# A four-layer perceiver in one launch: L1 and L2 self-attention written out tile by tile, and the L0 alignment and L0 attention reordered

## Time and profile before

| | |
|---|---|
| median of 3 runs | 4878.07 us (4868.13 to 4886.44) |
| the profiled execution | 4887.39 us, span 4885.7 us |
| mean granted TensorE clock | 0.884 of 2.4 GHz |
| busy: PE, PEld, DVE, ACT, POOL | 75%, 61%, 73%, 58%, 21% of the span |
| L0 cross attention (distances and alignment) | 17.2 to 486.1 us |
| L0 attention | 486.1 to 616.6 us |
| L1 attention | 1586.4 to 1735.3 us |
| L2 attention | 2736.6 to 2886.8 us |

### The profile page before, as it was taken

One profiled execution on the slowest core, in us unless ns is written; L12 is line 12 of the kernel. 1 busy time (PEld: TensorE's weight loads), 2 busy tenths in 40 slices (PEclk: granted clock), 3 DMA queues, 4 the chain that ended last, 5 costly groups with the idle time before them and its releaser, 6 DMA issues. The chain is left out here.

```text
span 4885.7 us, 68656 instructions
## 1 busy us (share of the span) xinstructions
PE 3687.9 (75%) x23747; PEld 2956.0 (61%) x23747; DVE 3576.9 (73%) x5812; ACT 2810.2 (58%) x4595; POOL 1036.9 (21%) x993
## 2 busy tenths in 40 slices
PE   6236617999999567999999765777777777777775
PEld 3235315999998345899999532555555555555664
DVE  4675776787776432877787447999999999997443
ACT  3112404666665322666666314998988999997112
POOL 0000402111210200221111111444434444443000
PEclk9556757999999779999999877999999999998777
DMA  7452001111110001111110001000000000000000
GB/s 272 69 81 70 1 5 59 35 35 35 35 35 9 7 18 61 34 35 34 36 35 21 9 5 37 14 24 18 14 14 28 14 14 28 14 8 19 1 0 15
DMA packets 182323, 158.33 MB, mean 32 GB/s; under 512 B 7340, under 2 KB 170364, under 8 KB 182012
## 3 DMA queue, kind: packets, MB, share of 16 engines
q1 hardware_dynamic: 175356, 138.02, 10.2%
q10 hardware_dynamic: 6656, 16.38, 1.1%
HBM read 127.62 MB, written 20.20 MB: 30 GB/s over the span
## 5 line engine op out<-in xcount | busy, mean ns | idle before, releaser
L537 PEld LDWEIGHTS psU<-ctxN,ST 128*128 128x128 f32 x6656 | 853.8, 191 | 98.0 <-issue 39.2
L537 PE MATMUL psU<-ctxN,ST 128*128 128x129 f32 x6656 | 868.0, 275 | 20.5 <-issue 20.5
L1159 DVE MAX8 top<-pairs 128x8 f32<-128x801 f32 (+1 forms) x512 | 709.1, 1406 | 4.5
L623 ACT ACTIVATE ST<-ST 128x512 f32<-128x512 f32 (+1 forms) x832 | 513.3, 625 | 166.9 <-DVE ST L725 162.9
L934 PE MATMUL psU<-ctxN,PT 128*128 128x129 f32 (+1 forms) x3328 | 432.9, 281 | 201.2 <-ACT PT L1042 201.1
L1124 POOL TENSOR_TENSOR P<-P,EX 128x1601 f32<-128x1601 f32 x128 | 459.5, 3589 | 586.8 <-ACT P L1034 586.8
L725 DVE TENSOR_TENSOR ST<-ST,psB 128x512 f32<-128x512 f32 (+1 forms) x832 | 556.2, 677 | 3.3 <-PE psB L556 3.3
L711 DVE TENSOR_TENSOR psA<-psA,ST 128x512 f32<-128x512 f32 x640 | 446.5, 698 | 136.7 <-ACT ST L615 69.6
L934 PEld LDWEIGHTS psU<-ctxN,PT 128*128 128x128 f32 (+1 forms) x3328 | 395.3, 193 | 225.5 <-ACT PT L1042 225.5
L1164 DVE MATCH_REPLACE8 pairs<-top,pairs 128x801 f32<-128x801 f32 (+1 forms) x384 | 482.3, 1256 | 0.0
L912 PE MATMUL psS<-KT,stat 128*128 128x512 f32 (+1 forms) x1024 | 389.4, 524 | 15.9 <-DVE pairs L1143 15.1
(11 more groups left out here) (459 smaller groups left out, 6731.6 us busy)
## 6 DMA issues: line engine op xcount, KB each, us to landing
ctxT<-ctxT_scratch SPq DMA_DIRECT2D x48, 800.5 KB, 4.7
ctxN<-in_ctx SPq DMA_DIRECT2D x48, 768.0 KB
ctxT_scratch<-trn ACTq DMA_DIRECT2D x16, 800.5 KB
nat<-in_ctx SPq DMA_DIRECT2D x16, 768.0 KB
ctx<-in_ctx SPq DMA_DIRECT2D x16, 768.0 KB
dist_scratch<-dd SPq DMA_DIRECT2D x8, 800.5 KB
room<-dcol SPq DMA_DIRECT2D x28, 201.0 KB, 4.2
dcol<-dist_scratch SPq DMA_DIRECT2D x16, 201.0 KB, 16.7
```

The lines of the kernel that those rows point to most:

```text
L537: last = pe.matmul(psU[:, q, 0:D + 1], ST[0:n, i % SLOTS, q * 128:q * 128 + 128], ctxN[0:n, j, k, 0:D + 1], start=(k == 0 and q % 2 == 0), ...
L623: act.activation(ST[0:n, i % SLOTS, :], ST[0:n, i % SLOTS, :], ACT.Exp).then_inc(exp_done, 1)
L1159: dve.max(top[:, j, 8 * n:8 * n + 8], pairs[:, j, 0:width]).then_inc(listed, 1)
```

## The change

1. **Distances**: for a group of 512 columns PE first issues the token products of both batches, then waits once for both squares, then issues the two matmuls of ones.
2. **Alignment, opening**: only the parts of `dcol` that no DMA fills are set to zero, all by DVE. Of POOL's work only `top` stays in the opening block; `same_batch`, `iota_far` and `place` go to POOL in the block of the steps.
3. **Alignment, rows**: one ring of 36 rows and one more. `carry_row` is run once, at step 36, in place of 17 times.
4. **Alignment, last sums**: the two batches of a tile take turns, product by product, into the two halves of the partitions.
5. **L0 attention**: the keys of tile t+2 go ahead of `mix(t)` on POOL; ACT negates the maxima; ACT copies the values, behind `key_squares(1)`, in place of DVE; POOL makes `group_rows`; DVE takes key and query forms half by half; the first dots and denominators go ahead of the values on PE; each waits for its half of the queries only. For the last tile DVE multiplies, masks, finds the maximum and subtracts it, and ACT takes one exponential for 8 heads.
6. **L1 attention** has a function of its own, `attention_gelu`, and **L2 attention** another, `attention_wide_values`, both written out for 8 tiles, with scores two tiles ahead, three buffers of `P`, and the keys spread over 8 groups of heads on two halves of the partitions. In L2 the weights are applied to x itself (4 matmuls a tile, 64-row stationary, 512 columns), and the weight is multiplied once a tile (16 matmuls, accumulated). In L1 the heads are summed transposed, so gelu takes its bias from the partition and feeds the projection directly; two tiles share a gelu. Half of the products need x or V with its two batches exchanged, which SP makes by DMA. L3 keeps `small_attention`.

```diff
 # distances
                         for j in range(2):
                             b = 2 * p + j
-                            r = slice(j * S, j * S + S)
-                            pe.wait_ge(squared, b + 1 + ONE)
-                            pe.matmul(psD[r, n, 0:w], xm2[:, b * S:b * S + S], trn[:, b % TURNS, o:o + w],
+                            pe.matmul(psD[j * S:j * S + S, n, 0:w], xm2[:, b * S:b * S + S], trn[:, b % TURNS, o:o + w],
                                       start=True, stop=False)
-                            last = pe.matmul(psD[r, n, 0:w], c.ones[:, 0:S], trn_sq[:, b % TURNS, o:o + w],
+                        pe.wait_ge(squared, 2 * p + 2 + ONE)
+                        for j in range(2):
+                            b = 2 * p + j
+                            last = pe.matmul(psD[j * S:j * S + S, n, 0:w], c.ones[:, 0:S], trn_sq[:, b % TURNS, o:o + w],
                                              start=False, stop=True)
 # alignment
-                    dve.memset(dcol[:, 0:STEPS // 2, :], 0.0).then_inc(filled, 1)
+                    dve.memset(dcol[:, 0:BLOCKS - 1, :], 0.0).then_inc(filled, 1)
+                    dve.memset(dcol[:, S:STEPS, :], 0.0).then_inc(filled, 1)
+                    dve.memset(dcol[:, BLOCKS - 1:S, 0:1], 0.0).then_inc(filled, 1)
+                    dve.memset(dcol[96:128, BLOCKS - 1:S, 1 + FROM[-1][1]:ROWS + 1], 0.0).then_inc(filled, 1)
...
-                            if s % G == 0 and s:
-                                pe.wait_ge(row_carried, s // G + ONE)
+                            if s == RING:
+                                pe.wait_ge(row_carried, 1 + ONE)
...
-                for b in range(B):
...
+                for p in range(NT):
...
                     for k, (o, w) in enumerate(KC):
                         pe.wait_ge(inside_ready, g * len(KC) + k + 1 + ONE)
-                        last = pe.matmul(psX[r, b // 2, :], inside[0:w, k, b * S:b * S + S], ctx[0:w, b, k, :],
-                                         start=(k == 0), stop=(k == len(KC) - 1))
+                        for j in range(2):
+                            b = 2 * p + j
+                            last = pe.matmul(psX[j * S:j * S + S, p, :], inside[0:w, k, b * S:b * S + S],
+                                             ctx[0:w, b, k, :], start=(k == 0), stop=(k == len(KC) - 1))
 # L0 attention: POOL, then ACT
-                for t in range(NT):
-                    mix(t)
+                for t in range(NT - 1):
                     if t + 2 < NT:
                         keys(t + 2)
+                    mix(t)
...
+                def negate(t):
+                    act.wait_ge(max_found, t + 1 + ONE)
+                    act.activation(nmx[:, t % 2, :], mx[:, t % 2, :], ACT.Copy, scale=-1.0).then_inc(neg_ready, 1)
 # L2 attention, new: PE's order, and two of its steps
+                def values(t):
+                    pe.wait_ge(pt_ready, 2 * t + 2 + ONE)
...
+                    for b in range(2):
+                        for e in range(2):
+                            n = 2 * b + e
...
+                            x = c.xn if b == e else swapped
+                            pe.matmul(u_bank(n), x[rows(e), t, :], PT[rows(e), t % 2, :, rows(b)], start=True, stop=True
+                                      ).then_inc(u_ready, 1)
+
+                def output(t):
+                    pe.wait_ge(ut_ready, 4 * t + 4 + ONE)
...
+                    for h in range(H):
+                        last = pe.matmul(psY[:], UT[:, t % 2, h // 2, h % 2].rearrange("p b s -> p (b s)"), W[:, h, :],
+                                         start=(h == 0), stop=(h == H - 1))
...
+                scores(0)
+                scores(1)
+                for t in range(NT):
+                    if t + 2 < NT:
+                        scores(t + 2)
+                    turn(t)
+                    if t:
+                        output(t - 1)
+                    values(t)
+                output(NT - 1)
 # L1 attention, new: the sums of a tile, PE's loop, DVE's two passes and DVE's loop
+                    for a in range(8):
+                        for b in range(2):
+                            for e in range(2):
+                                h = 2 * a + e
+                                v = V if b == e else swapped
+                                r = slice(h % 4 * 32, h % 4 * 32 + 32)
+                                last = pe.matmul(psO[r, h // 4, t % 2, rows(b)], v[rows(e), t, h * 32:h * 32 + 32],
+                                                 PT[rows(e), t % 2, a, rows(b)], start=True, stop=True)
...
+                for t in range(NT):
+                    if t + 2 < NT:
+                        scores(t + 2)
+                    turn(t)
+                    if t + 2 < NT:
+                        values(t + 2)
+                    if t >= 3 and t % 2:
+                        output(t - 3)
+                        output(t - 2)
+                    sums(t)
...
+                    dve.tensor_tensor(p, psS[:].rearrange("p g (h k) -> p (g h) k", k=S), bc(mask[:], [128, H, S]), ALU.add
+                                      ).then_inc(masked, 1)
...
+                    dve.reduce_max(m[:, :, 0], p, axis=X).then_inc(max_ready, 1)
...
+                    dve.tensor_tensor(p, p, bc(m, [128, H, S]), ALU.subtract).then_inc(sub_ready, 1)
...
+                    dve.reduce_sum(m[:, :, 0], p, axis=X).then_inc(sum_ready, 1)
...
+                    dve.reciprocal(m[:, :, 0], m[:, :, 0]).then_inc(inv_ready, 1)
...
+                    dve.tensor_tensor(p, p, bc(m, [128, H, S]), ALU.mult).then_inc(p_ready, 1)
...
+                for t in range(NT):
+                    if t + 2 < NT:
+                        shift(t + 2)
+                    if t + 1 < NT:
+                        weigh(t + 1)
+                    if t >= 3 and t % 2:
+                        add(t - 3)
+                        add(t - 2)
```

More of the change, by code:

```diff
@@ L1852, in _ @@
                     project(n)
-                values(0)
-                values(1)
                 dots(0)
@@ L1857, in _ @@
                     far(0, part)
-                values(2)
-                values(3)
+                for p in range(4):
+                    values(p)
                 for i in range(NT + 4):
@@ L1918, in _ @@
                 key_squares(1)
+                for p in range(4):
+                    values(p)
                 for i in range(NT + 2):
                     if 0 <= i - 2:
+                        if i - 2 < NT - 1:
+                            negate(i - 2)
                         exps(i - 2, 0)
@@ L1988, in add @@
                     dve.tensor_tensor(c.x[:, t, :], c.x[:, t, :], psY, ALU.add).then_inc(y_added, 1)
-                key(0)
-                key(1)
-                query_forms(0)
-                query_forms(1)
-                dve.wait_ge(mask_ready, 1 + ONE)
-                dve.tensor_copy(group_rows[:], bc(group_mask[:], [128, G, S])).then_inc(q_forms, 1)
-                values(0)
-                values(1)
+                for n in range(2):
+                    key(n)
+                    query_forms(n)
                 for i in range(NT + 4):
@@ L2783, in batch, with ring @@
                     return s // G % 2, s % G
+                def ring(s):
+                    return s % RING
                 @block.sync
@@ L2855, in _ @@
                         if s < STEPS:
-                            if s % G == 0 and s:
-                                carry_row(s // G)
+                            if s == RING:
+                                carry_row()
                             set_edge(s)
```

487 lines of the change are left out of this document (412 added, 75 removed).

## The result

The changed kernel takes **4709.1 us**, median of 4 runs (4708.0 to 4716.0), against 4882.3 for the kernel before (4 runs): a ratio of 0.9647, 95% interval 0.9624 to 0.9670. The forecast was 4721, the range 4685 to 4768. The profiled executions have spans of 4885.7 and 4714.3 us, 171.4 apart.

| stage | before | forecast | after |
|---|---|---|---|
| L0 cross attention | 468.9 | 442 | 444.4 |
| L0 attention | 130.5 | 107 | 109.9 |
| L1 attention | 148.9 | 92 | 88.6 |
| L2 attention | 150.1 | 100 | 87.0 |
| the eight others | 3970.0 | unchanged | 3967.3 |

What follows compares the result with a forecast made beforehand. L0, L1 and L2 attention had no full engine; L1 and L2 were two-lane loops waiting on each other, L0 was DVE-bound. Terms -9.8 - 6.7 - 10.5 - 23 - 57 - 50 = -157 gave 4721 us, range 4685 to 4768.

Steps and rivals of the forecast that it cites:

- the alignment: In L0 cross attention: opening -9.8 us, row copies -6.7, last sums by turns -10.5.
- L0 attention: Stage forecast -23 us (-13 to -30), with periods of 9.3 us between reciprocals and a shorter tail.
- the tail: L0 attention from the last reciprocal to the end, 29.2 us before: estimated gain 4.5 us, between 0 and 8.
- L1 attention: Stage forecast -57 us (-45 to -69), 92 and not 149, PE setting the pace at 8.3 us a tile.
- the sums: L1 attention, 64 records a tile on PE: taken as 3.1 us, between 2.2 and 4.1.
- L2 attention: Stage forecast -50 us (-38 to -62), 100 and not 150, PE setting the pace at 9.6 us a tile.
- The weights on x: L2 attention, 4 matmuls of 512 columns a tile: taken as 3.0 us, between 1.8 overlapped and 3.5 in turn.
- PE is faster than I count: Rival: sums overlap, clock at upper level, DVE sets the pace; L1 -69, L2 -62, total 4694 us; chance 0.15.
- PE at half clock: Rival: PE at half clock half the time; L1 -33, L2 -12, L0 attention -15, alignment -25, total 4793; chance 0.13.
- POOL holds DVE up: Rival: POOL's keys delay DVE passes in L1 (5 to 10 us) and L2 (perhaps 3); total 4732 us; chance 0.08.
- the rule on two SBUF inputs: DVE instruction with two SBUF inputs contends with GpSimd reading SBUF, second blocked in full; two of DVE's five passes exposed.
- A stage outside changes by more than 3 us: Sign that the forecast is wrong: a stage outside the four touched ones changes by more than 3 us.

Runs made afterwards that it cites:

- u1: Changed kernel with PE's old order in the distances only; 4716.3 us.
- u6: Changed kernel; in L0 attention DVE divides, copies and adds for tiles 5, 4 and 3 ahead of its passes over the last tile; 4708.1 us.
- u11: Changed kernel with u6, one L1 projection a tile and, third order, PE turning half the last tile's weights ahead of O of tile 6; 4705.7 us.
- u9: Changed kernel, but DVE in place of ACT negates the maxima in L0 attention (tiles 0 to 6); 4704.5 us.
- u10: Kernel before with the changes of the distances, the alignment and L0 attention only, L1 and L2 attention as before; 4847.4 us.
- u12: Changed kernel with runs of four products in the alignment's last sums (per batch) and L1 attention's sums (per array quarter); 4722.1 us.
- u4: Changed kernel; L1 attention's sums of a tile issued by column quarter, eight products in a row, in place of by turns; 4742.5 us.
- u3: Changed kernel; L2 attention's products of weights on x issued two of one row half, then two of the other; 4717.2 us.

## Why the prediction was right

**Right, with its steps.** The direction, the four places and the alignment. From the last root on the alignment lost 27.6 us, against 9.8 + 6.7 + 10.5 = 27.0. From that root to the first scan it takes 34.0 us (before 161.78 - 118.19 = 43.6): 9.6 for the opening. From the first scan to the last it takes 160.9 us (before 167.6): 6.8 for the row copies. Behind the last scan it takes 145.5 (before 156.6): 11.2, and the last sums are 11.1 by their own experiment. The whole stage came to 444.4 and not 442, since the distances ended 3 us later; whether their new order did that is open (u1).

**L0 attention, 20.6 where I said 23.** Two errors nearly cancelled, which is luck. The second reciprocal starts 26.5 us after the start of the stage (I had 26.9), but from it to the last it took 52.1 us and not 6 x 9.3 = 56: with keys ahead DVE runs at its bound in four of the six periods (7.55, 8.22, 8.42, 8.42, where I had 8.65), and only 10.14 and 9.34 are longer. The step that failed is the tail: I forecast 4.5 us less, it became 2.1 longer (31.2 against 29.1), because DVE's new passes for the last tile stand ahead of its division for tile 5, and PE's turning of tile 6 behind that. I had priced the passes but not asked what is queued behind them. Moving them behind the division gives back 3.5 of the 6.5 us that the tail missed (u6), the third order of u11 another 1.8; the remaining 1.2 us stay open.

**L1 attention, 60.3 where I said 57.** The pace is DVE's and not PE's: 6.32 us where I had 8.3. The mis-sized term is the sums, 3.1 us forecast and 1.12 measured; by turns over the parts of the array they take almost a third of what they take in runs of eight products (3.18). I had taken the price of a row with no such turns. What gave part of it back is one period of 12.54 and a wait at the end, from one result buffer for two projections; I had counted one wait a tile and not this.

**L2 attention, 63.2 where I said 50.** PE does set the pace, 7.53 us a tile where I had 9.6. The weights on x took 1.9 and not 3.0 us: the two row halves overlap, and I had taken the value nearer to no overlap. Turning took 1.09 and not 1.32, and no wait was left. The first projection is added 34.5 us after the start of the stage. The lesser errors have the same sign. My guess is that each item was cheaper on a PE at work without gaps than in a kernel full of waits; no run tests it.

**The rivals.** The time came out between my forecast and the rival "PE is faster than I count" (4694), which described L1 and L2 attention rightly (-69 and -62) except for the buffer. "PE at half clock" is partly true: the granted clock is 0.79 and 0.84, and 3 of 8 tiles in L1 have sums of 1.95 us. "POOL holds DVE up" was seen, 1.65 us in one pass, but without POOL's additions the stage was only 0.6 us shorter, within its scatter. The negation, which I took there as a case of the rule on two SBUF inputs, has one, so the rule as I gave it does not cover it; that it waits for POOL's pass to end is what the trace shows (u9). Of my signs, PE busy over 80% in L1 attention (66%), a clock of 0.9 in L1 and L2 attention (0.79 and 0.84) and a record of sums of 0.05 us (0.0175 at full clock) were wrong, and the periods of L0 attention are 8.7 us in the mean and not 9.3. "A stage outside changes by more than 3 us" happened: L1's feed-forward part (-4.7) and L3 attention (+4.1); the first goes with the change (u10); the second lies within the scatter of that stage.

## What to carry to other kernels

When an order is written out by hand, list for each step that you move or add what stands behind it on its engine and who waits for that: the two losses here (5.75 and 3.77 us of PE waiting) both came from a quick step behind DVE's long turn, and putting it ahead gave back 3.5 and 9.9 us. Issue small products by turns over the parts of the array, and price them by a row that is issued so. A producer that others wait for (the keys) goes ahead of a consumer (mixing): with this alone undone the stage was 18.7 us longer, nearly all that it had gained.

## What the runs showed of the hardware

**A stage that nobody changed sets the scatter.** L3 attention took 277.5, 291.7, 295 to 296 or 307 us in the fourteen profiled executions. It has four rounds, and in each PE makes the same 256 records of narrow products (64 and 16 moving columns) in a row. These take 14.5 to 15.4 us where the granted clock is 0.93 to 1.00 and 26.3 us where it is 0.50. The third round, in the changed kernel and in that of u9:

```profile
4501.40:4527.70 26.30, 26.30 (x259) 26.30 (x260) 4.69 (x6) 0.00 (x0) 0.00 (x0) 0.50 0.00 0
```

```profile
4499.60:4515.00 15.40, 15.40 (x259) 15.38 (x260) 4.70 (x6) 0.00 (x0) 0.00 (x0) 0.93 0.00 0
```

So in these 26.3 us PE was busy throughout, with 1.2 GHz granted. Of the four rounds none was at half clock in the stage of 277.5 us, one in each of the ten of 291.7 to 295.9, and two in each of the three of 307. What decides which round stays at half clock was not found; small differences in whole times of this kernel should be read from the stages.

**Overlap of parts of the array depends on the order and on the size of the products.** The same 32 products of L1 attention take 1.12 us by turns (changed kernel), 2.40 in runs of four (u12) and 3.18 in runs of eight (u4), all at full clock. In L2 two products of the same row half in a row cost PE nothing (1.92 us both ways, u3), since it started the other half's product beside the first.

**A short DVE instruction can be held up for longer than it takes itself.** The negation of 16 columns, 0.17 us without POOL at work, took 1.41 to 1.43 beside a pass of POOL that had begun 1 us earlier, and ended 0.03 us behind that pass each time (523.19 and 523.16 in u9). ACT did the same in 0.22 beside the same pass of POOL.
